# All four low halves of the experts on GpSimd, the bias product ahead of a transpose, and a first weighing in quarters: a float32r FFN with adapters on one Trainium2 core

## What is computed

```python
# layer 1: x is [8, 128, 512], one adapter (rank 16) of 32 per sequence
base_out = einsum('bti,oi->bto', x, W) + b
h   = base_out + einsum('btr,bro->bto', einsum('bti,bir->btr', x, A[slot]), Bm[slot]) * 2.0
# layer 2: 16 experts of rank 64, top 2
base_out   = einsum('bsi,oi->bso', h, base_w) + base_b
res_hidden = einsum('bsi,ri->bsr', h, A2)                 # 64 numbers per token
probs      = softmax(einsum('bsi,ei->bse', h, router_w))  # 16 experts
topw, topi = top_k(probs, 2);  topw /= topw.sum() + 1e-6
combine    = sum(one_hot(topi) * topw)
delta      = einsum('bse,bsr,eor->bso', combine, res_hidden, B) * 0.5
return x + base_out + delta
```

## Time and profile before

| | value |
|---|---|
| time, median of 3 runs | 103.99 us (103.42 to 104.17) |
| time of the profiled execution | 102.98 us |
| span of the profile (first to last instruction) | 101.2 us |
| TensorE (PE), matmuls busy | 97.4 us, 96% of the span |
| VectorE (DVE) busy | 66.5 us, 66% |
| ScalarE (ACT) busy | 41.4 us, 41% |
| GpSimd (POOL) busy | 21.3 us, 21% |
| mean granted TensorE clock | 1.000 |

### The profile page before, as it was taken

The page is one execution under the profiler, slowest core; times in us unless marked ns, Lnnn a source line. Parts: engine busy times, 40 slices in busy tenths (PEclk is TensorE's granted clock), DMA queues, the critical chain, the costliest instruction groups (busy, mean ns, idle before and its releaser), DMA issues.

```text
span 101.2 us, 1808 instructions
## 1 busy us (share of the span) xinstructions
PE 97.4 (96%) x572; PEld 88.1 (87%) x572; DVE 66.5 (66%) x184; ACT 41.4 (41%) x100; POOL 21.3 (21%) x34
## 2 busy tenths in 40 slices
PE   6999999999999999999999999999999999999990
PEld 7799999999999899789988997899787787788980
DVE  5729996999389776949917946676468626648101
ACT  1705445878768626554344127110910603012000
POOL 5100002243999970070430050000000000000000
PEclk9999999999999999999999999999999999999999
DMA  2999459999955083386196091470074091750211
GB/s 42 362 363 378 138 111 313 366 410 424 314 118 97 23 220 66 115 185 196 23 254 219 16 266 37 126 198 3 16 188 141 5 268 60 216 198 0 104 58 52
DMA packets 8155, 16.92 MB, mean 167 GB/s; under 512 B 1539, under 2 KB 3971, under 8 KB 8018
## 3 DMA queue, kind: packets, MB, share of 16 engines
q1 hardware_dynamic: 7474, 16.41, 53.2%
q10 hardware_dynamic: 640, 0.40, 1.3%
q0 software_dynamic: 32, 0.00, 0.0%
HBM read 13.28 MB, written 2.16 MB: 153 GB/s over the span
## 4 chain that ended last, share of the span: by engine, by line
PE 93%; DMA 3%; DVE 0%; ACT 0%; issue 0%
PE pair L804 89%; DMA w_raw_all<-w_cat 3%; PE pair L963 1%; PE pair L943 1%; PE pair L945 1%; DVE xn L798 0%; PE pair L920 0%; ACT w_hi_all L416 0%; PE pair L933 0%; PE pair L922 0%; PE pair L912 0%
## 5 line engine op out<-in xcount | busy, mean ns | idle before, releaser
L804 PE MATMUL pair<-e_hi,w_hi_all 128*128 128x512 f32 (+1 forms) x72 | 27.3, 379 | 0.0
L804 PE MATMUL pair<-e_hi,w_lo_all 128*128 128x512 f32 (+1 forms) x72 | 26.7, 370 | 0.0
L804 PE MATMUL pair<-e_lo,w_hi_all 128*128 128x512 f32 (+1 forms) x72 | 26.6, 370 | 0.0
L742 DVE TENSOR_TENSOR exp_raw_all<-w_raw_all 128x512 f32<-128x512 f32 x16 | 10.3, 687 | 10.7 <-DMA w_raw_all<-spill 10.7
L526 ACT ACTIVATE w_hi_all<-exp_raw_all 128x512 fp32r<-128x512 f32 x16 | 9.7, 629 | 15.8 <-DVE exp_raw_all L742 15.8
L804 PEld LDWEIGHTS pair<-e_hi,w_lo_all 128*128 128x128 f32 x72 | 13.6, 188 | 2.5
L804 PEld LDWEIGHTS pair<-e_hi,w_hi_all 128*128 128x128 f32 x72 | 13.6, 189 | 2.4
L804 PEld LDWEIGHTS pair<-e_lo,w_hi_all 128*128 128x128 f32 x72 | 13.6, 189 | 1.8
L749 DVE TENSOR_TENSOR w_lo_all<-exp_raw_all,w_hi_all 128x512 fp32r<-128x512 f32 x16 | 10.4, 689 | 3.1 <-ACT w_hi_all L526 2.5
L804 PE MATMUL pair<-p_hi,w_hi_all 128*128 128x304 f32 x32 | 9.8, 307 | 0.0
L804 PE MATMUL pair<-p_hi,x_hi 128*128 128x304 f32 x32 | 9.8, 305 | 0.0
(11 more groups left out here) (106 smaller groups left out, 166.9 us busy)
## 6 DMA issues: line engine op xcount, KB each, us to landing
w_raw_all<-spill SPq DMA_DIRECT2D x16, 256.0 KB, 3.9
exp_raw_all<-experts SPq DMA_DIRECT2D x4, 512.0 KB, 8.4
xn<-x_n SPq DMA_DIRECT2D x4, 512.0 KB, 7.4
out<-xn SPq DMA_DIRECT2D x7, 256.0 KB, 3.9
w_raw_all<-w_cat SPq DMA_DIRECT2D x3, 552.0 KB, 7.0
xt_raw<-x_t SPq DMA_DIRECT2D x2, 512.0 KB, 7.0
xt_raw<-x_t SPq DMA_DIRECT2D x1, 1024.0 KB, 12.4
c_stack<-c_hi SPq DMA_DIRECT2D x7, 74.0 KB, 4.4
```

Of the source, the lines that this page charges most:

```text
L742: nc.vector.tensor_tensor(g[:, js, :], weight_rows[:, b, js, :], hidden[:, b, :].unsqueeze(1).to_broadcast([P, GH, P]), ALU.mult).then_inc ...
L804: return nc.tensor.matmul(out_ap, lhs, rhs, start=first, stop=last)
```

## The change

1. GpSimd makes part 2 of `e_lo` too: its order becomes part 0, A parts of tile 3, part 1, part 2, A parts of tile 4, x low half of tile 4, part 3. VectorE's `split_experts_lo(2)` and its semaphore are gone.
2. `bias()` stands ahead of `lora_first_transpose()` on TensorE, and the copy of the bias row ahead of the copy of the transposed values on ScalarE.
3. The first tile's weighing is made in four pieces of 256 columns instead of two of 512: `weigh_first`, `g_lo_first` (VectorE) and `g_hi_first` (ScalarE). TensorE waits for them at chunks 0, 2, 4 and 6 instead of 0 and 4.
4. The high half of the weights' row block `k` = 1 is made in two ScalarE instructions of 256 columns instead of one of 512. TensorE waits for the first at `m` = 0 and for the second at `m` = 2.

```diff
@@ GpSimd
             split_experts_lo(1)
+            split_experts_lo(2)
+            lora_a_parts(4)
+            x_lo_part(4)
+
             split_experts_lo(3)
-            for t in range(4, NT):
+            for t in range(5, NT):
                 lora_a_parts(t)
                 x_lo_part(t)
@@ ScalarE
-            for k in range(1, KC):
+            act.wait_ge(in_w[1], 16)
+            for cols, done in ((W_LEFT, wh_next), (W_RIGHT, wh_done)):
+                nc.scalar.activation(w_hi[:, 1, cols], w_raw[:, 1, cols], ACT.Copy).then_inc(done, 1)
+            for k in range(2, KC):
...
+            def g_hi_first():
+                for q in range(4):
+                    js = slice(q * GH // 2, (q + 1) * GH // 2)
+                    if q % 2:
+                        act.wait_ge(g_done, q // 2 + 1)
+                    else:
+                        act.wait_ge(g_piece, q // 2 + 1)
+                    nc.scalar.activation(gt_hi[:, 0, js, :], g[:, js, :],
+                                         ACT.Copy).then_inc(gh_done if q % 2 else gh_piece, 1)
...
             first_rows()
-            lora_first_t()
             act.wait_ge(pe_bias, 1)
             nc.scalar.activation(bias_hi[F_BIAS:FT, :], w2_cols(ps_b)[F_BIAS:FT, :], ACT.Copy).then_inc(bh_done, 1)
+            lora_first_t()
             split_experts(1)
...
@@ VectorE
+            def weigh_first():
+                dve.wait_ge(doubled[0], 16)
+                dve.wait_ge(spread[0], 32)
+
+                dve.wait_ge(el_pool_done, 1)
+                for q in range(4):
+                    js = slice(q * GH // 2, (q + 1) * GH // 2)
+                    nc.vector.tensor_tensor(g[:, js, :], weight_rows[:, 0, js, :],
+                                            hidden[:, 0, :].unsqueeze(1).to_broadcast([P, GH // 2, P]),
+                                            ALU.mult).then_inc(g_done if q % 2 else g_piece, 1)
+                    if q:
+                        g_lo_first(q - 1)
+                g_lo_first(3)
+
+            def g_lo_first(q):
+                js = slice(q * GH // 2, (q + 1) * GH // 2)
+                if q % 2:
+                    dve.wait_ge(gh_done, q // 2 + 1)
+                else:
+                    dve.wait_ge(gh_piece, q // 2 + 1)
+                nc.vector.tensor_tensor(gt_lo[:, 0, js, :], g[:, js, :], gt_hi[:, 0, js, :].bitcast(F32),
+                                        ALU.subtract).then_inc(gl_done if q % 2 else gl_piece, 1)
...
             route(0)
-            split_experts_lo(2)
             lora_lo(2)
...
             route(2)
-            weigh(0, 0)
-            weigh(0, 1)
-            g_lo(0, 0)
-            g_lo(0, 1)
+            weigh_first()
             lora_lo(4)
@@ TensorE
             for k in range(1, KC - 1):
-                pe.wait_ge(wh_done, k + 1)
                 pe.wait_ge(wh_first, k + 2)
                 for m in range(KC):
+                    if k == 1 and m == 0:
+                        pe.wait_ge(wh_next, 1)
+                    elif m == (KC // 2 if k == 1 else 0):
+                        pe.wait_ge(wh_done, k + 1)
                     fold_pass(m, k, w_hi, w_hi, False, False)
...
             x_other(0)
+            bias()
             lora_first_transpose()
-            bias()
             x_first(1)
```

More of the change, by code:

```diff
@@ L197, in adaln_ffn_kernel @@
         wh_left = sem("wh_left")
+        wh_next = sem("wh_next")
         wh_done = sem("wh_done")
@@ L216, in adaln_ffn_kernel @@
         el_pool_done = sem("el_pool_done")
-        el_done = sem("el_done")
         consts = sem("consts")
@@ L253, in adaln_ffn_kernel @@
         gl_done = sem("gl_done")
+        g_piece = sem("g_piece")
+        gh_piece = sem("gh_piece")
+        gl_piece = sem("gl_piece")
         pe_d = sem("pe_d")
@@ L553, in _ @@
             routing_rows(1)
-            g_hi(0, 0)
-            g_hi(0, 1)
+            g_hi_first()
             lora_hi(4)
@@ L634, in folded_lo @@
                                         p_hi[:, m, R:MVN].bitcast(F32), ALU.subtract).then_inc(pl_done, 1)
-            def split_experts_lo(q):
-                js = slice(q * GC // 4, (q + 1) * GC // 4)
-                dve.wait_ge(eh_done, q + 1)
-                nc.vector.tensor_tensor(e_lo[:, js, :], exp_raw[:, js, :], e_hi[:, js, :].bitcast(F32),
-                                        ALU.subtract).then_inc(el_done, 1)
             x_lo_early(0)
@@ L734, in weigh @@
                     dve.wait_ge(spread[b], 32 * (t // NB + 1))
-                    if t == 0:
-                        dve.wait_ge(el_pool_done, 1)
-                if t >= 1:
-                    dve.wait_ge(gh_done, 2 * (t - 1) + half + 1)
-                    dve.wait_ge(gl_done, 2 * (t - 1) + half + 1)
+                dve.wait_ge(gh_done, 2 * (t - 1) + half + 1)
+                dve.wait_ge(gl_done, 2 * (t - 1) + half + 1)
                 nc.vector.tensor_tensor(g[:, js, :], weight_rows[:, b, js, :],
@@ L967, in experts_product @@
                 for c in chunks:
-                    if c in (0, GH):
-                        pe.wait_ge(gh_done, 2 * t + (1 if c == 0 else 2))
-                        pe.wait_ge(gl_done, 2 * t + (1 if c == 0 else 2))
-                    if t == 0 and c in (2, 6):
-                        pe.wait_ge(el_pool_done, 2 if c == 2 else 3)
-                    if t == 0 and c == 4:
-                        pe.wait_ge(el_done, 1)
+                    if t == 0 and c in (0, GH):
+                        pe.wait_ge(gh_piece, 1 if c == 0 else 2)
+                        pe.wait_ge(gl_piece, 1 if c == 0 else 2)
+                    elif c == (GH // 2 if t == 0 else 0) or c == (GH + GH // 2 if t == 0 else GH):
+                        pe.wait_ge(gh_done, 2 * t + (1 if c < GH else 2))
+                        pe.wait_ge(gl_done, 2 * t + (1 if c < GH else 2))
+                    if t == 0 and c in (2, 4, 6):
+                        pe.wait_ge(el_pool_done, c // 2 + 1)
                     for n, (lhs, rhs) in enumerate(((gt_hi, e_hi), (gt_hi, e_lo), (gt_lo, e_hi))):
```

## The result

The changed kernel takes 103.53 us (median of 14 runs, 103.02 to 104.37). The kernel before, 14 times beside it, takes 103.25 us (102.19 to 104.80). The ratio is 1.0055, 95% interval 1.003 to 1.0079: slower by about 0.57 us (0.28 between the two medians; the ratio compares runs of the same round, and its interval is 0.31 to 0.82 us). The forecast shift was +0.6 us; the forecast level, 104.6 us, was 1.1 us too high.

A forecast was written before the change was run, and what follows sets the result against it. TensorE's matmul list plus its gaps was taken as the bound. Start -0.05, lock +0.1 and quarters +0.58 gave +0.63 us, added as 0.6 to the median 103.99: 104.6 us, range 103.3 to 105.3.

The forecast's parts named there:

- D: TensorE's gap ahead of routing_transpose(2), 0.31 us before the change, inferred to be ended by VectorE's lora_lo(4).
- D moves as forecast: Likeliest case: the wait ahead of routing_transpose(2) ends +0.3 to +1.0 us later, 104.3 to 105.0 us; chance 0.58.
- A: TensorE's gap of 0.24 us ahead of lora_first_product; the bias order was to shrink it by 0.14.
- B: TensorE's gap of 0.27 us ahead of x_first(3); moving part 2 of e_lo off VectorE was to close it.
- C: TensorE's gap of 0.13 us ahead of the first experts' chunk; the quarters were to close it.
- Start of the weighing, −0.05: VectorE's first weighing, begun at a DMA's landing, was to start 0.05 us earlier; bounds -0.14 and +0.15.
- The lock, +0.1: VectorE's first weighing was to find GpSimd's A parts instruction running and lose 0.1 us; bounds 0 to 0.6.
- The rival that part 3 runs into the weighing: GpSimd's part 3 still runs and holds VectorE's first piece up to 2.4 us: 105.1 to 107 us; chance 0.11.
- GpSimd undisturbed: Without VectorE's overlapping part, GpSimd's part 2 of e_lo was to run undisturbed, from about 31.7 to 34.1 us.
- The block k = 1: Making this weights' block's high half in two was to gain TensorE at most 0.2 us; taken as 0.
- The sum: routing_transpose(2) freed later by -0.05 (start) + 0.1 (lock) + 0.58 (quarters) = +0.63 us.
- The level: The forecast total: the median 103.99 us plus the shift 0.6, giving 104.6 us.

The follow-up runs named there:

- e1: The changed kernel with lora_hi(4) and lora_lo(4) ahead of the first weighing's work on ScalarE and VectorE: 102.3 us, ratio 0.9931 to the kernel before.
- e2: The changed kernel with the first weighing in two halves of 512 columns again: 103.11 us, ratio 1.0001 to the kernel before.
- e6: The kernel before with only the bias product ahead of the transpose, on TensorE and ScalarE: 103.18 us, ratio 0.9973.
- e10_quarters_between_only: The kernel before with only the first weighing in quarters and lora_hi(4), lora_lo(4) between its pieces: 102.46 us, ratio 0.9942.
- e9_block_one_only: The kernel before with only the high half of the weights' block k = 1 in two pieces: 103.0 us, ratio 0.9974.
- e4_halves_adapter_first: The changed kernel with the weighing in halves and the adapter's parts of tile 4 ahead of it: 103.05 us, ratio 1.0014 to the kernel before.

## Why the prediction was right and wrong, point by point

- *The bounds and the stalls.* Right. TensorE's list with its four gaps accounts for the difference: the stretch behind `routing_transpose(2)` is constant to 0.2 us, and in the profiles a kernel is as much shorter as the stalls that it closes. One more place can stall: the weights' block `k` = 1, without a gap in the profile of before, stalled TensorE for 0.5 to 0.7 us in the profiles of `e1`, `e2` and `e6`. TensorE's arrival at D, 40.8 + 3 x 0.24 = 41.5, was added up 0.13 too late (the chunk's first two loads stand 0.11 apart, 41.33 and 41.44); nothing in the sum rests on it.
- *D moves as forecast* (the likeliest case, +0.3 to +1.0). It happened. The transpose was forecast at 42.9; it starts at 42.31, and with the head start of 0.63 that is 42.94. The pieces take 3.34 us from the weighing's start to the end of `lora_lo(4)`, forecast 3.36. The steps inside fit as well: pieces in a row start 0.34 apart (0.33 forecast), and there are two bubbles. One stands ahead of 39.66, where 38.75 + 2 x 0.34 = 39.43 would do, the other in the last pair's 0.99 us, where two in a row take 0.76: 0.23 us each, 0.25 forecast. The quarters alone give the whole loss, and with halves the changed kernel is level with before.
- *A, B, C.* A shrank by 0.09 where 0.14 was forecast, B and C are gone, and all of it is waited away at D, as forecast (D went from 0.31 to 1.51: the 0.71 by which the transpose is later, and the 0.49 by which TensorE comes earlier).
- *Start of the weighing, −0.05.* This term was mis-sized. Counted from the start of the block the weighing begins at 14.33 instead of 14.08, so the term is +0.25: `routing_transpose(0)` comes 0.12 earlier, and from there to the weighing it takes 0.37 more (8.11 against 7.74). Part 1 of the change was suspected, since this distance is 7.93 or more in each kernel with it, and 7.74 to 7.89 in three without it; but `e10_quarters_between_only` has 8.20 and `e9_block_one_only` 9.01 without it. Within it, SyncE's issue of the spread stands 2.30 us behind that of the spill before (32.23 to 34.53), 2.58 after, and 2.58 in `e9_block_one_only`, which has nothing of part 1. One and the same kernel has 7.93 and 8.38 in its two profiles. So these DMAs vary by 0.3 to 0.5 us between executions, and whether GpSimd's order has a part in it stays open. The bounds given, −0.14 to +0.15, were too narrow.
- *The lock, +0.1.* It was 0: GpSimd's A parts end at 38.67, before the weighing at 38.75. It was a matter of 0.08 us in this profile. The rival that part 3 runs into the weighing did not happen; part 3 ends at 38.09, forecast 38.7 (the difference is the head start).
- *GpSimd undisturbed.* Right: its two parts take 4.78 us instead of 5.74 and the longest single one 2.41 instead of 3.19, now that VectorE's part is gone.
- *The block k = 1.* Taken at 0, at most 0.2. No ratio shows anything; 0.15 us in profiles where the block lands late is inside the bound.
- *The sum.* +0.63 stands against +0.71 in the profile and +0.57 by the ratio. That it comes so near is in part luck: the start was 0.30 too low, and the lock (0.10), the pieces (0.02) and the time from the end of `lora_lo(4)` to the load (0.10 shorter, taken as unchanged) were together 0.22 too high.
- *The level: the step that failed.* It is the last, "I add it to the median: 103.99 + 0.6". The median of three runs was 0.7 us above that of 14 (103.25), and 0.8 to 1.1 above the medians beside the experiments (102.93 to 103.18). So 104.6 us lies 1.35 above the kernel before as measured, and the changed kernel lies 0.28 above it by the medians and 0.57 by the ratio. With 103.25 as base the forecast is 103.85, still 0.3 above the 103.53 measured. The profiled execution, 102.98 us, would have given 103.6, but that is luck: it lies 0.27 below the median of 14. The reason given, that the shift is independent of the loads at the start, holds for the shift and says nothing on the level. It isn't quite true of the shift either: part of a head start can be given back, at the block `k` = 1 or where the spread or the bias rows land late (31.75 in `e4_halves_adapter_first`).

## What to carry to other kernels

Before work is cut finer so that its first piece comes sooner, look at what stands behind its last piece on the same engine: here two instructions of 16 columns stood there, the transpose waited for them, and their place was worth 1.2 to 1.6% (1.0055 to 0.9931 and 0.9893, each against the kernel before) where the cut had cost 0.5%. In these profiles, gains ahead of a stall that is set by another engine were worth nothing until that stall was gone; close the last one first. Compare two profiles by distances between events of the program, not by the time from the start, and put a small computed shift on a base with many runs.

## What was not expected of the hardware

- The distance of TensorE's matmuls of 296 columns falls from 0.25 to 0.135 us (1.2 and 2.2 columns per ns) at a time that lies between 4.5 and 8.7 us in the profiles of these kernels, and at 6.1 and 8.7 for one and the same kernel, at a granted clock that reads 1.00 throughout. The two rates lie near TensorE's two clock levels, 1.2 and 2.4 GHz. Ahead of it, in these two profiles, stand 13 matmuls of zeros (0.8 to 3.9 us) and then matmuls without a gap from 4.2 and 4.4 us on. What sets the time is not shown. Between those two profiles it moves the start of the block from 24.94 to 26.05 us; 0.23 of these 1.1 us are the later first matmul (4.21, 4.44).
- VectorE's instructions of 256 columns take 0.42 us but start 0.34 apart, those of 512 take 0.69 and start 0.60 apart: one instruction cut in two costs 0.07 us in a row of them (2 x 0.335 − 0.60), eight for four 0.28. The Trainium skill (VectorE: DVE Perf Modes, the TRN2 errata) gives (N + 151) / 0.96 ns; its 424 ns is the duration in the rows (0.42), but its fixed part, 157 ns, is not what a cut costs here, because instructions in a row overlap by 0.09. The other half of the 0.56 us by which the weighing grew is waiting for ScalarE: the two bubbles, 0.47 us, in the place of one of 0.19 before (39.13 + 2 x 0.60 = 40.33 to 40.52).
